# The tail of a graph layer and routed expert kernel: which adds wait for which, dense weights once for two graphs, and the order of the last 50 work items

## The chip, the cores and the metric

The kernel runs on one core of a Trainium2 chip. The metric is the device time of one execution in microseconds (us), as the median of several runs. A profiled execution of the same program is read beside it; all durations below come from that one.

## The reference, cut to what matters

16 graphs of 512 nodes with 128 features go through two residual layers. The first is a graph layer (convolutions along the nodes, an adjacency weighted message sum, gates). The second is a mixture of 8 experts with 2 chosen for each token:

```python
x = x + gnn(layernorm(x), adj, ...)
xn = layernorm(x) * gamma + beta
top_vals, top_idx = top_k(xn @ Wr + br, 2)
w = softmax(top_vals)
for e in range(8):
    h = gelu(xn @ W1[e] + b1[e])          # 128 -> 256
    y = y + (h @ W2[e] + b2[e]) * w_full[..., e]   # 256 -> 128
x = x + y
```

What is added to a token is the weighted output of its two experts.

## The kernel before

An iteration g from 0 to 15 computes the graph layer of graph g and ends that of graph g - 1 (residual sum, norm, router). The first 14 graphs are **routed**: GpSimd (POOL) scatters each token's row, with its weights and its own number, into the regions of its two experts in a DRAM tensor `routed`. Tiles of 256 rows (T0, T1, ...) are read back with the expert's weights, go through the expert, and POOL adds their results into `out` with indirect accumulating DMAs, two for a tile (L943 to L952). From g = 4 on, four such tiles are streamed in each iteration: T0 to T47.

Two tiles may hold the same token, and an accumulating DMA must not run beside another one on the same row. So `add` (L943) waits on POOL for the semaphore `added` to count all adds of all tiles before, for every tile.

The last two graphs (q = 0 and 1) are **dense**: all 8 experts run on all their tokens, and VectorE (DVE) adds weighted results to the graph's tile in SBUF, which SyncE (SP) stores at the end.

After the last iteration comes the **tail**, a list of 50 items that `last_items` (L350) writes out: 18 tiles (T48 to T65, `LAST`) and 32 dense items (graph q, expert e, half u of 256 tokens). Five tiles come first, then two dense items after each tile, then the dense items that are left. Item i passes through the engines as follows: a tile is transposed (`turn`), `hidden` multiplies by W1 on TensorE (PE), ScalarE (ACT) does gelu, `second` multiplies by W2 (L570), ACT adds the bias, `back` transposes, and DVE multiplies by the weights (`weigh`, `dense_weigh`), which raises `y_done`. At step i PE issues turn(i+2), hidden(i+1), second(i), back(i-1). Items alternate between two sets of PSUM banks (bank_set, by the number m of the item): H and Y for even items, G for odd ones.

Tile buffers (`xt`, `w1_t`, `w2_t`, `y_t`) form a ring of 8. The weights of a dense pair of items are in `wd1` and `wd2`, two buffers in turn; there are 16 such loads, one for each graph and expert, and each serves two items. SP issues all loads of the tail in one order that `loads_in_order` (L377) writes out. Before a tile's loads SP reads the tile's place and expert out of SBUF (`choice`, L418 to L420) and waits until the adds of the tile eight before it are done (L481); before a dense load it waits until the items of the load two before it are done (L424 to L426). SP is one queue: what waits there holds up all that follows.

The tables of places come from DVE (`table_steps`, L1157). The tail's own table (`LAST` entries) is made in iteration 15, in `t_start_last` and `t_expert_last`; SP waits for it (L472), stores 8 blocks of pad rows behind the experts' regions (L473 to L475) and then loads T48. With this input, counting the reference's choices, 13 of the 18 tail tiles hold tokens: 2, 1, 2, 1, 1, 2, 2 and 2 for the experts 0 to 7. The other 5 are filled with pad rows.

Of the kernel before, what the change touches and what calls it, by code (L numbers as in the profile page):

```python
# [47 lines left out]
ADD_ITEMS = 3  # L48
# [62 lines left out]
LAST_STEPS = 15  # L111
# [23 lines left out]
def pad_rows():  # L135

    r = np.zeros((SLOTS, TILE, ROW), np.float32)
    r[:, :, R_ID] = (TOKENS + np.arange(TILE)).astype(np.uint32).view(np.float32)
    return r.reshape(SLOTS * TILE, ROW)


def gnn_moe(nc, x, adj_t, weights, vectors, consts, pads, routed, w1_all, w2_all, out):
# [4 lines left out]
    with ExitStack() as ctx:  # L147
# [35 lines left out]
        late_end = sb("late_end", [P, 512])  # L183

# [65 lines left out]

        t_c = sb("t_c", [1, EXPERTS], I32)
# [14 lines left out]
        t_pad = sb("t_pad", [1, EXPERTS], I32)  # L266

# [82 lines left out]
        def last_items():  # L350


            dense = [(q, e, u) for q in range(DENSE) for e in range(EXPERTS) for u in range(NODES // TILE)]
# [10 lines left out]
        items = list(last_items())  # L364

# [25 lines left out]
        def _(sp):  # L391
# [16 lines left out]
            sp.dma_start(routed[DUMMY:DUMMY + SLOTS * TILE, :], pads).then_inc(pads_stored, 16)  # L408
            sp.dma_start(out[TOKENS:TOKENS + TILE, :], pads[0:TILE, 0:P]).then_inc(out_set, 16)
# [8 lines left out]
            def choice(table, i):  # L418
                at = sp.value_load(t_start[table][0:1, i:i + 1], min_val=0, max_val=DUMMY + (SLOTS - 1) * TILE)
                e = sp.value_load(t_expert[table][0:1, i:i + 1], min_val=0, max_val=EXPERTS - 1)  # L420
                return at, e

            def dense_loads(k):
                if k >= 2:  # L424
                    sp.wait_ge(pe_y, last_of_load(k - 2) + 1)
                    sp.wait_ge(yT_done, last_of_load(k - 2) + 1)  # L426
                e = k % EXPERTS
# [49 lines left out]
            sp.wait_ge(pads_stored, 16 * (EXPERTS + 1))  # L477
# [13 lines left out]
            for q in range(DENSE):  # L491
                sp.wait_ge(y_done, last_of_load((q + 1) * EXPERTS - 1) + 1)
# [259 lines left out]
        def _(act):  # L752
# [156 lines left out]
            number = {item[1]: item[0] for item in items if is_tile(item)}  # L909
# [25 lines left out]
        def _(pool):  # L935
# [7 lines left out]
            def add(n, m=None):  # L943
                j = n % RING
                pool.wait_ge(y_done, (n if m is None else m) + 1)
                if n > 0:
                    pool.wait_ge(added, 16 * TT * n)
                for t in range(TT):
# [3 lines left out]
                        in_=y_t[j][:, t, :], in_offset=None, compute_op=ALU.add).then_inc(added, 16)  # L952

            def iteration(g, tail, more, moe):
# [41 lines left out]
            pool.wait_ge(out_set, 16 * (ROUTED + 1))  # L996
            for item in items:
                if is_tile(item):
                    add(item[1], item[0])

        @block.vector
        def _(dve):
# [154 lines left out]
            def table_steps(d, tiles, table):  # L1157
# [18 lines left out]
                def tables(beside):  # L1176
# [7 lines left out]
                    if every:  # L1184
# [12 lines left out]
                                                 over(t_e[:, 0:tiles], 2, s_e1), ALU.is_equal), beside=beside)  # L1197
                    step(nc.vector.tensor_tensor(oh, oh, over(t_z[:], 1, s_e1), ALU.mult), beside=beside)
                    step(nc.vector.tensor_reduce(t_s[:, 0:tiles], oh, AX.X, ALU.add), beside=beside)
                    if every:  # L1200
                        step(nc.vector.tensor_tensor(t_s[:, 0:tiles], t_s[:, 0:tiles], steps, ALU.add), beside=beside)
                        step(nc.vector.tensor_scalar(start[:], t_s[:, 0:tiles], float(DUMMY), None, ALU.min),
                             wait=False)
# [32 lines left out]

            def weigh(n, m=None):
                m = n if m is None else m
                dve.wait_ge(pe_yT, m + 1)
                dve.wait_ge(own_done, n + 1)  # L1240
                nc.vector.tensor_tensor(y_t[n % RING][:],  # L1241
                                        YO[bank_set(m)][:, TILE:2 * TILE].rearrange("p (t d) -> p t d", t=TT),
# [220 lines left out]
            sums = {}  # L1463
            for i in range(-2, len(items) + 1):
                if i + 2 < len(items) and is_tile(items[i + 2]):
                    m, n, j, loads = items[i + 2]
                    tile_lo(n, bank_set(m))
                    own_weight(n, j, loads)
# [87 lines left out]
```

## Time and profile before

| what | value |
|---|---|
| time, median of 3 runs | 682.06 us (680.07 to 682.51) |
| time of the profiled execution | 677.4 us |
| its span in the profile | 675.6 us |
| TensorE busy | 623.9 us (92% of the span) |
| VectorE, ScalarE, GpSimd busy | 493.2, 417.7, 339.4 us |
| adds of tiles on GpSimd (L949) | 132, mean 1623 ns each |
| idle time of GpSimd before them | 189.8 us, of it 98.7 us for an earlier add to land |
| tail, first transpose of T48 to the last transpose | 546.5 to 666.2 us |
| mean granted TensorE clock | 0.98 of full speed |

The span is what the profiler saw of the program's instructions; 1.8 us of the execution lie around it. A line such as L949 is a line of the kernel before. "Releaser" is the instruction or DMA that ended a wait; "issue" is idle time for which the profile shows no releaser.

### The profile page before, as it was taken

The page shows a single profiled execution, that of the slowest core. Times are in us where ns is not written, and L with a number is a line of the kernel's source. Part 1 is how long each engine was busy: PE and PEld are TensorE (multiplying, and loading weights), DVE is VectorE, ACT ScalarE, POOL GpSimd, SP SyncE. Part 2 cuts the span into 40 slices and gives each one's busy share as a digit, 9 for nine tenths or more (in the row PEclk, how much of TensorE's full clock was granted, in tenths as well). Part 3 has the DMA queues.
Part 4 walks back from the last instruction along what each step waited for, and adds up shares of the span by engine and source line. Part 5 has one row for each costly group of instructions (what it writes and reads, how often), then busy time and mean ns, then how long its engine had stood idle before and what let it go on. Part 6 is the DMA issues. An engine that isn't in the chain of part 4 may idle for free.

```text
span 675.6 us, 12962 instructions
## 1 busy us (share of the span) xinstructions
PE 623.9 (92%) x3784; PEld 529.7 (78%) x3784; DVE 493.2 (73%) x2028; ACT 417.7 (62%) x824; POOL 339.4 (50%) x255
## 2 busy tenths in 40 slices
PE   3799897999999999999999999999999988898993
PEld 2779586788888888888888888888888867787872
DVE  6958878778888888888888888888878755333321
ACT  4554445385858585858585858585858556465661
POOL 3100404044757474757484847485748435354554
PEclk9899898999999999999999999999999999899997
DMA  8227231445574757564757565656565586666543
GB/s 299 93 90 251 77 118 50 133 144 159 139 183 126 178 130 180 127 183 124 172 135 177 131 175 132 173 133 175 134 169 137 124 213 156 155 164 160 125 87 60
DMA packets 102710, 99.14 MB, mean 147 GB/s; under 512 B 9056, under 2 KB 80480, under 8 KB 102368
## 3 DMA queue, kind: packets, MB, share of 16 engines
q1 hardware_dynamic: 80048, 81.39, 39.2%
q0 software_dynamic: 22592, 16.92, 16.6%
q8 instruction: 31, 0.51, 0.3%
q14 instruction: 39, 0.32, 0.2%
HBM read 73.97 MB, written 26.21 MB: 148 GB/s over the span
## 4 chain that ended last, share of the span: by engine, by line
PE 80%; DVE 11%; issue 3%; DMA 2%; ACT 2%; POOL 1%; POOLq 0%; SPq 0%; DVEq 0%; ACTq 0%
PE Y L570 9%; PE C L502 9%; PE C L503 8%; PE C L504 8%; PE G L678 7%; PE G L502 5%; PE G L504 4%; PE G L503 4%; PE G L570 3%; PE H L545 2%; PE H L546 2%; PE H L547 2%; PE Y L578 2%; PE G L533 2%; PE M L508 2%
## 5 line engine op out<-in xcount | busy, mean ns | idle before, releaser
L949 POOL DMA_INDIRECT out<-y_t,xt x132 | 214.3, 1623 | 189.8 <-DMA out<-y_t,xt 98.7
L964 POOL DMA_INDIRECT routed<-row,at_u x112 | 116.4, 1040 | 126.8 <-DVE at_u L1152 96.4
L502 PE MATMUL C<-cv_h,w_hi 128*128 128x256 f32 (+1 forms) x432 | 133.2, 308 | 8.9 <-DVE cv_l L1013 7.5
L503 PE MATMUL C<-cv_l,w_hi 128*128 128x256 f32 (+1 forms) x432 | 125.9, 291 | 0.0
L504 PE MATMUL C<-cv_h,w_lo 128*128 128x256 f32 (+1 forms) x432 | 125.5, 290 | 0.0
L502 PEld LDWEIGHTS C<-cv_h,w_hi 128*128 128x128 f32 x432 | 84.1, 195 | 14.9 <-DVE cv_l L1013 9.9
L503 PEld LDWEIGHTS C<-cv_l,w_hi 128*128 128x128 f32 x432 | 84.1, 195 | 1.3
L504 PEld LDWEIGHTS C<-cv_h,w_lo 128*128 128x128 f32 x432 | 84.0, 194 | 0.7
L570 PE MATMUL Y<-ge,w_t 128*128 128x256 f32 x228 | 61.5, 393 | 3.6 <-DVE y_t L1241 1.6
L678 PE MATMUL G<-ex,msg_t 128*128 128x512 f32 x128 | 58.9, 603 | 0.3 <-ACT gh L871 0.3
L570 PEld LDWEIGHTS Y<-ge,w_t 128*128 128x128 f32 x228 | 39.4, 192 | 21.2 <-issue 17.9
L773 ACT ACTIVATE ge<-H,w_t 128x256 f32<-128x256 f32 x114 | 47.8, 472 | 6.0 <-PE H L547 4.2
L678 PEld LDWEIGHTS G<-ex,msg_t 128*128 128x128 f32 x128 | 23.1, 191 | 23.5 <-issue 22.9
L502 PE MATMUL G<-xlT_h,w_hi 128*128 128x512 f32 x96 | 39.9, 415 | 1.5 <-DVE xlT_l L1083 1.5
L880 ACT CAST cv_h<-G 128x512 fp32r<-128x512 f32 x16 | 9.4, 586 | 50.8 <-PE G L678 50.8
L1348 DVE TENSOR_TENSOR ex<-ex,adj 128x512 f32<-128x512 f32 x64 | 39.8, 680 | 0.0
L504 PE MATMUL G<-xlT_h,w_lo 128*128 128x512 f32 x96 | 38.4, 400 | 0.0
L503 PE MATMUL G<-xlT_l,w_hi 128*128 128x512 f32 x96 | 38.1, 396 | 0.0
L545 PE MATMUL H<-xT_h,w_t 128*128 128x256 f32 x114 | 35.8, 314 | 0.7 <-DVE xT_l L1225 0.7
L781 ACT ACTIVATE yT<-Y,w_t 128x256 f32<-128x256 f32 x57 | 27.1, 475 | 11.9 <-PE Y L570 11.0
L1083 DVE TENSOR_TENSOR xlT_l<-M,xlT_h 128x512 fp32r<-128x512 f32 x16 | 11.1, 692 | 30.3 <-ACT xlT_h L801 30.3
L547 PE MATMUL H<-xT_h,w_t 128*128 128x256 f32 x114 | 32.2, 282 | 0.0
(250 smaller groups left out, 1637.6 us busy)
## 6 DMA issues: line engine op xcount, KB each, us to landing
w_t<-w_all SPq DMA_DIRECT2D x66, 256.0 KB, 4.2
adj<-adj_t SPq DMA_DIRECT2D x16, 1024.0 KB, 5.7
xt<-routed SPq DMA_DIRECT2D x66, 144.0 KB, 3.3
w_t<-w_all SPq DMA_DIRECT2D x66, 136.0 KB, 3.7
x_ln<-x SPq DMA_DIRECT2D x16, 256.0 KB, 6.1
x_res<-x SPq DMA_DIRECT2D x16, 256.0 KB, 6.6
wd<-w_all SPq DMA_DIRECT2D x16, 256.0 KB, 3.9
out<-x SPq DMA_DIRECT2D x15, 256.0 KB
```

What stands on the lines that cost most here:

```text
L502: pe.matmul(psum, hi(w), rhs_h, start=start, stop=False)
L503: pe.matmul(psum, hi(w), rhs_l, start=False, stop=False)
L504: return pe.matmul(psum, lo(w), rhs_h, start=False, stop=stop)
L545: pe.matmul(half, w[:, h * P:(h + 1) * P], x_h, start=True, stop=False)
L547: last = pe.matmul(half, w[:, (2 + h) * P:(3 + h) * P], x_h, start=False, stop=True)
L570: last = pe.matmul(YO[bank_set(m)][:, 0:TILE], w2[:, h * P:(h + 1) * P], ge[m % 2][:, h, :], start=(h == 0), stop=(h == HALVES - 1))
L678: last = pe.matmul(G0[:], msg_t[:, j, :], ex[:, j, :], start=(j == 0), stop=(j == NT - 1))
L773: last = nc.scalar.activation(ge[m % 2][:, h, :], HID[bank_set(m)][:, h * TILE:(h + 1) * TILE], ACT.Gelu, bias=w2[:, X_B1 + h:X_B1 + h + 1])
L781: nc.scalar.activation(yT[m % 2][:], YO[bank_set(m)][:, 0:TILE], ACT.Identity, bias=w2[:, X_B2:X_B2 + 1]).then_inc(yT_done, 1)
L949: nc.gpsimd.indirect_dma_start(out=out, out_offset=bass.IndirectOffsetOnAxis(ap=xt[j][:, t, R_ID:R_ID + 1].bitcast(U32), axis=0), in_=y_t[ ...
L964: nc.gpsimd.indirect_dma_start(out=routed, out_offset=bass.IndirectOffsetOnAxis(ap=at_u[:, n:n + 1], axis=0), in_=row[:, n // TOP, :], in_ ...
L1348: nc.vector.tensor_tensor(ex[:, j, :], ex[:, j, :], adj[:, j, :], ALU.mult).then_inc(a_prod, 1)
```

## The change

**Adds wait for other experts' tiles only.** The tail's tiles are in order of their expert. A token is at most once in one expert's region, so two tiles of one expert never touch the same row. In the tail, `last_add` waits for the count of adds that stood before the first tile of its own expert. That count is worked out on DVE (five table steps more and one less, `LAST_STEPS` 19 in place of 15), lies in `t_run`, and POOL reads the 18 values into registers in iteration 15, 9 ahead of the add of T46 and 9 behind it. Before each pair of adds there is a small POOL operation. All pad tiles wait for all real ones. As pad tiles may now be added side by side, they have rows of their own: `pads` grows from 1024 to 4608 rows, and `out` from 256 to 4608 rows behind the tokens. Three quarters of that (3584 rows of 576 bytes in `routed` and 3584 of 512 bytes in `out`) are stored by SP in iteration 5, from DRAM to DRAM.

**Results and row numbers get buffers of their own.** `y_last` gives each of the 18 tiles its own place (in `adj`, `ex` and `x_ln`, which are free by then), and `take_places` on DVE copies a tile's row numbers to `ids`. So the ring's buffers are free once PE, ACT and DVE have read them: from T56 on, SP waits for those in place of the adds.

**Dense weights are loaded once for both graphs.** 10 loads in place of 16: experts 0 and 1 for graph 0, experts 2 to 7 for both graphs (four items each), and experts 0 and 1 for graph 1.

**One and two dense items to a tile in turn.** T65 is item 37 of 0 to 49 (before: item 43), with 12 dense items behind it. The loads of T56 to T60 now stand ahead of the third dense load in SP's order; before it was those of T56 and T57. The lists, with d for a dense item and the number of its load:

```
before: T48 T49 T50 T51 T52 d0 d0 T53 d1 d1 T54 d2 d2 T55 d3 d3 ... T65 d13 d13 d14 d14 d15 d15
after:  T48 T49 T50 T51 T52 d0 d0 T53 d1 T54 d1 d2 T55 d2 T56 d2 d2 ... T65 d6 d6 d6 d6 d7 d7 d7 d7 d8 d8 d9 d9
```

```diff
-ADD_ITEMS = 3
+EARLY = 2
+DENSE_LOADS = ([(e, (0,)) for e in range(EARLY)] + [(e, (0, 1)) for e in range(EARLY, EXPERTS)] +
+               [(e, (1,)) for e in range(EARLY)])
...
-                    for q, e, u in dense[k:k + 2]:
-                        yield m, q, e, u, k // 2
+                    for entry in dense[k:k + 1 + n % 2]:
+                        yield m, *entry
...
-            at = [(last_of_load(k - 2), 1, k) for k in range(2, DENSE * EXPERTS)]
-            at += [(STREAMED + ADD_ITEMS * (n - RING - STREAMED + 1), 0, n) for n in range(STREAMED, STREAMED + LAST)]
+            at = [(last_of_load(k - 2), 1, k) for k in range(2, len(DENSE_LOADS))]
+            at += [(number.get(n - RING, STREAMED), 0, n) for n in range(STREAMED, STREAMED + LAST)]
...
+                if g == FIRST + 1:
+                    sp.dma_start(routed[DUMMY + TAKEN:, :], pads[TAKEN:, :]).then_inc(pads_stored, 16)
+                    sp.dma_start(out[TOKENS + TAKEN:, :], pads[TAKEN:, 0:P]).then_inc(pads_stored, 16)
...
             def last_loads(n):
                 at, e = choice(2, n - STREAMED)
-                sp.wait_ge(added, 16 * TT * (n - RING + 1))
+                if n < STREAMED + RING:
+                    sp.wait_ge(added, 16 * TT * (n - RING + 1))
+                else:
+                    sp.wait_ge(pe_y, number[n - RING] + 1)
+                    sp.wait_ge(yT_done, number[n - RING] + 1)
+                    sp.wait_ge(own_done, n - RING + 1)
...
+            def load_starts(a, b):
+                for i in range(a, b):
+                    run_starts.append(pool.value_load(t_run[0:1, i:i + 1], min_val=16 * TT * STREAMED,
+                                                      max_val=16 * TT * (STREAMED + LAST)))
+            def last_add(n, m):
+                i = n - STREAMED
+                pool.wait_ge(y_done, m + 1)
+                pool.wait_ge(added, run_starts[i])
+                nc.gpsimd.tensor_tensor(pool_spare[:, i:i + 1], cst[:, 0:1], cst[:, 1:2], ALU.add)
+                for t in range(TT):
+                    nc.gpsimd.indirect_dma_start(
+                        out=out, out_offset=bass.IndirectOffsetOnAxis(ap=ids[:, i, t:t + 1], axis=0),
+                        in_=y_last[i][:, t, :], in_offset=None, compute_op=ALU.add).then_inc(added, 16)
...
+                if d == ROUTED:
+                    pool.wait_ge(tab_step, TAB_STEPS * (ROUTED - 2) + LAST_STEPS)
+                    load_starts(0, LAST // 2)
                 tile_add(2)
...
+                if d == ROUTED:
+                    load_starts(LAST // 2, LAST)
...
+                    if every:
+                        step(nc.vector.tensor_tensor(t_f[:, 0:EXPERTS], t_cum[:], t_a[:], ALU.subtract), wait=False)
+                        step(nc.vector.tensor_copy(t_f[:, EXPERTS:], t_cum[:, EXPERTS - 1:]), beside=beside)
+                        step(nc.vector.tensor_tensor(t_of[:], oh, over(t_f[:], 1, s_e1), ALU.mult), beside=beside)
+                        step(nc.vector.tensor_reduce(t_r[:], t_of[:], AX.X, ALU.add), beside=beside)
+                        step(nc.vector.tensor_scalar(t_run[:], t_r[:], 16 * TT / TILE, float(16 * TT * STREAMED), ALU.mult,
+                                                     ALU.add), wait=False)
...
+            def take_places(n, j, loads):
+                dve.wait_ge(xt_in[j], loads)
+                nc.vector.tensor_copy(ids[:, n - STREAMED, :], xt[j][:, :, R_ID].bitcast(U32))
```

## Rows read from the trace of the kernel before

**Rows 1.** The chain that ended last: start us, us, what.

```profile
662.05 1.55 POOL out L949
...
663.91 3.47 DMA out<-y_t,xt
...
668.13 1.55 POOL out L949
```

**Rows 2.** GpSimd in order of time: start us, us; idle time in brackets.

```profile
544.72 1.55 POOL L949 DMA_INDIRECT out<-y_t,xt  x1 [4.01 <-DVE y_t L1241]
...
551.18 1.55 POOL L949 DMA_INDIRECT out<-y_t,xt  x1 [3.06 <-DMA out<-y_t,xt]
```

**Rows 3.** Line L147, sequencers at the end: durations in ns, starts.

```profile
L147 POOLq DRAIN  x1: 7002/7002/7002, 668.4 to 668.4; - x1
```

**Rows 4.** Line L495, SyncE's last wait: when it was over.

```profile
L495 SPq EVENT_SEMAPHORE  x1: 17/17/17, 673.2 to 673.2; - x1
```

**Rows 5.** All engines in order of time, the last microseconds.

```profile
666.35 0.61 DVE L1255 SCALAR_TENSOR_TENSOR x<-G,w_d,x 128x128 f32<-128x128 f32 x2 [0.17 <-PE G L578]
666.99 0.39 SPq L493 DMA_DIRECT2D out<-x  x1
```

**Rows 6.** SyncE in order of time, a graph's store in iteration 14.

```profile
486.50 0.40 SPq L447 DMA_DIRECT2D out<-x  x1
```

**Rows 7.** GpSimd in order of time, the add that this store released.

```profile
488.67 1.64 POOL L949 DMA_INDIRECT out<-y_t,xt  x1 [0.30 <-DMA out<-x]
```

**Rows 8.** SyncE in order of time, its issues at the tail's start.

```profile
540.05 0.41 SPq L412 DMA_DIRECT2D xt<-routed  x1
...
556.52 0.38 SPq L412 DMA_DIRECT2D xt<-routed  x1
...
570.57 0.38 SPq L412 DMA_DIRECT2D xt<-routed  x1
...
572.09 0.37 SPq L428 DMA_DIRECT2D wd<-w_all  x1
```

**Rows 9.** VectorE in order of time, the tail's table in iteration 15.

```profile
524.26 0.32 DVE L1198 TENSOR_TENSOR t_oh<-t_oh,t_z 1x162 f32<-1x162 f32 x1
...
524.61 0.31 DVE L1199 TENSOR_REDUCE t_s<-t_oh 1x18 f32<-1x162 f32 x1
```

**Rows 10.** TensorE in order of time, idle times ahead of dense items.

```profile
576.22 0.55 PE L545 MATMUL G<-xd_h,wd 128*128 128x256 f32 x1 [1.76 <-issue]
...
610.86 0.36 PE L545 MATMUL H<-xd_h,wd 128*128 128x256 f32 x1 [0.95 <-issue]
...
631.12 0.36 PE L545 MATMUL G<-xd_h,wd 128*128 128x256 f32 x1 [0.76 <-issue]
...
659.07 0.35 PE L545 MATMUL H<-xd_h,wd 128*128 128x256 f32 x1 [0.73 <-issue]
```

**Rows 11.** Windows: PE, PEld, DVE, ACT, POOL busy us; PEclk, DMA share, GB/s.

```profile
577.00:578.00 1.00, 1.00 (x5) 0.97 (x5) 0.00 (x0) 0.07 (x1) 0.17 (x1) 0.50 0.07 16
```

**Rows 12.** Line L419, SyncE's reads of the table: ns.

```profile
L419 SPq TENSOR_LOAD <-t_start_last x18: 262/272/279, 538.7 to 620.7; - x18
```

**Rows 13.** GpSimd's groups: busy us, mean ns | idle us before.

```profile
L989 POOL TENSOR_TENSOR rs<-ve,cst 128x4 f32<-128x4 f32 x1 | 1.0, 1018 | 2.1 <-DVE ve L1036 2.1
```

**Rows 14.** Page, part 3: queue, packets, MB, share of 16 engines.

```profile
q1 hardware_dynamic: 80048, 81.39, 39.2%
```

**Rows 15.** Windows of iterations 5 and 6, columns as in Rows 11.

```profile
203.00:209.00 6.00, 5.86 (x31) 4.73 (x31) 4.07 (x12) 4.56 (x9) 4.24 (x5) 1.00 0.73 216
209.00:215.00 6.00, 6.00 (x48) 5.67 (x47) 5.73 (x12) 5.05 (x11) 5.09 (x4) 1.00 0.29 37
```

**Rows 16.** SyncE in order of time, tile loads of iteration 6.

```profile
230.54 0.39 SPq L412 DMA_DIRECT2D xt<-routed  x1
```

**Rows 17.** DMA issues in 11 to 30 us: KB, us to landing.

```profile
routed<-pads SPq DMA_DIRECT2D x1, 576.0 KB, 10.1
```

**Rows 18.** DMA issues in 526 to 540 us.

```profile
routed<-pads SPq DMA_DIRECT2D x8, 144.0 KB, 2.5
```

More of the change, by code:

```diff
@@ L248, in gnn_moe @@
         at_u = sb("at_u", [P, NT * 2], U32)
+        y_last = [tile[:, t, h * TILE:(h + 1) * TILE].rearrange("p (t d) -> p t d", t=TT)
+                  for tile in (adj, ex) for t in range(NT) for h in range(NODES // TILE)]
+        y_last += [x_ln[:, t:t + TT, :] for t in range(0, NT, TT)]
+        ids = sb("ids", [P, LAST, TT], U32)
         t_c = sb("t_c", [1, EXPERTS], I32)
@@ L266, in gnn_moe @@
         t_pad = sb("t_pad", [1, EXPERTS], I32)
+        t_f = sb("t_f", [1, EXPERTS + 1])
+        t_of = sb("t_of", [1, LAST, EXPERTS + 1])
+        t_r = sb("t_r", [1, LAST])
+        t_run = sb("t_run", [1, LAST], I32)
         parts = {
@@ L350, in last_items @@
         def last_items():
-            dense = [(q, e, u) for q in range(DENSE) for e in range(EXPERTS) for u in range(NODES // TILE)]
+            dense = [(q, e, u, k) for k, (e, graphs) in enumerate(DENSE_LOADS) for q in graphs
+                     for u in range(NODES // TILE)]
             m, n, k = STREAMED, STREAMED, 0
@@ L359, in last_items @@
                 if n > STREAMED + SPACED or n == STREAMED + LAST:
-                    for q, e, u in dense[k:k + 2]:
-                        yield m, q, e, u, k // 2
+                    for entry in dense[k:k + 1 + n % 2]:
+                        yield m, *entry
                         m, k = m + 1, k + 1
         items = list(last_items())
+        number = {item[1]: item[0] for item in items if len(item) == 4}
         def bank_set(m):
@@ L418, in choice @@
             def choice(table, i):
-                at = sp.value_load(t_start[table][0:1, i:i + 1], min_val=0, max_val=DUMMY + (SLOTS - 1) * TILE)
+                at = sp.value_load(t_start[table][0:1, i:i + 1], min_val=0, max_val=DUMMY + (LAST - 1) * TILE)
                 e = sp.value_load(t_expert[table][0:1, i:i + 1], min_val=0, max_val=EXPERTS - 1)
@@ L491, in _ @@
             for q in range(DENSE):
-                sp.wait_ge(y_done, last_of_load((q + 1) * EXPERTS - 1) + 1)
+                sp.wait_ge(y_done, max(item[0] for item in items if not is_tile(item) and item[1] == q) + 1)
                 sp.dma_start(out_v[ROUTED + q], x1_d[q][:]).then_inc(out_set, 16)
@@ L908, in _ @@
             results(STREAMED - 1, w2_t[(STREAMED - 1) % RING])
-            number = {item[1]: item[0] for item in items if is_tile(item)}
             for i in range(-2, len(items)):
@@ L941, in w_lo_part, with add @@
                                         ALU.subtract).then_inc(w_lo_done[name], 1)
-            def add(n, m=None):
+            def add(n):
                 j = n % RING
-                pool.wait_ge(y_done, (n if m is None else m) + 1)
+                pool.wait_ge(y_done, n + 1)
                 if n > 0:
@@ L996, in _ @@
             pool.wait_ge(out_set, 16 * (ROUTED + 1))
+            pool.wait_ge(pads_stored, 16 * (EXPERTS + 3))
             for item in items:
                 if is_tile(item):
-                    add(item[1], item[0])
+                    last_add(item[1], item[0])
         @block.vector
@@ L1200, in tables @@
                     if every:
-                        step(nc.vector.tensor_tensor(t_s[:, 0:tiles], t_s[:, 0:tiles], steps, ALU.add), beside=beside)
-                        step(nc.vector.tensor_scalar(start[:], t_s[:, 0:tiles], float(DUMMY), None, ALU.min),
-                             wait=False)
+                        step(nc.vector.tensor_tensor(start[:], t_s[:, 0:tiles], steps, ALU.add), wait=False)
                         assert done[0] == LAST_STEPS
@@ L1463, in _ @@
             sums = {}
+            dve.wait_ge(pe_nmp, GRAPHS)
             for i in range(-2, len(items) + 1):
@@ L1467, in _ @@
                     tile_lo(n, bank_set(m))
+                    take_places(n, j, loads)
                     own_weight(n, j, loads)
@@ L1548 @@
     args = [nc.dram_tensor(n, t.shape, F32, kind="ExternalInput").ap() for n, t in arrays.items()]
-    routed = nc.dram_tensor("routed", (DUMMY + SLOTS * TILE, ROW), F32, kind="Internal").ap()
+    routed = nc.dram_tensor("routed", (DUMMY + LAST * TILE, ROW), F32, kind="Internal").ap()
     w1_all = nc.dram_tensor("w1_all", (EXPERTS, P, W1COLS), F32, kind="Internal").ap()
     w2_all = nc.dram_tensor("w2_all", (EXPERTS, P, XCOLS), F32, kind="Internal").ap()
-    out = nc.dram_tensor("out", (TOKENS + TILE, P), F32, kind="ExternalOutput").ap()
+    out = nc.dram_tensor("out", (TOKENS + LAST * TILE, P), F32, kind="ExternalOutput").ap()
     gnn_moe(nc, *args, routed, w1_all, w2_all, out)
```

22 lines of the change are left out of this document (12 added, 10 removed).

## The prediction

> **What bounds the kernel now.** I read the chain that ended last from its end, then the engines' order of time over the tail. The span does not end with arithmetic. VectorE ends its last dense item at 666.35 + 0.61 = 666.96 us, and SyncE stores the graph at 666.99 [rows 5]. The chain's last links are adds on GpSimd: issue, 3.47 us until it lands, the next tile's issue at 668.13 [rows 1]. GpSimd's sequencer then sits in its final drain until 668.4 + 7.0 = 675.4 [rows 3], 2.2 us after SyncE's own last wait at 673.2 [rows 4], and the span ends at 675.6. So the end is set by a string of adds in which each waits for the one before: T47's starts at 551.18 [rows 2] and T65's at 668.13 [rows 1], so 18 tiles take 116.95 us, 6.50 us each. Behind this, by only 6 us, runs a second bound: TensorE with the 50 items. It is busy nearly all the time, but it stands still ahead of some dense items: 1.76 us at 576.22, then 0.95 and 0.76 us with two more (0.48 and 0.55 us) between them, and 0.73 us near the end [rows 10]. The profile calls these "issue". I read them as waits for dense weights: the first ends at 576.22, 4.1 us after SyncE issued that load at 572.09 [rows 8, 10], and four of the others come behind a dense load that stood in SyncE's queue behind a tile's load, which waited for adds.
>
> **The change part by part.** All sums are made against the profiled execution: 677.4 us, span 675.6. The median of the runs shown is 682.06, 4.7 us above it; I take the difference in span over to the median as it is.
>
> *Adds.* With this input 9 tiles of 18 begin an expert's run or the pad tiles (T48, T50, T51, T53, T54, T55, T57, T59, T61) and still wait, at 6.50 us each. The other 9 need only POOL's own time, two issues of 1.55 us with 0.3 us ahead of each, 3.7 us. From T47's 551.18 that is 9 x 6.50 + 9 x 3.7 = 91.8 us: T65's add at 643.0 at the earliest. The small operation ahead of each pair is not in the trace; it lies between 0 and the 1.02 us of a POOL operation on 128x4 [rows 13], so up to 18 us more, 661. T65's result itself is 12 items from the end, so at about 666.96 - 12 x 2.09 = 641.9 (the pace is worked out below). From T65's issue to the end of the drain were 675.4 - 668.13 = 7.3 us [rows 1, 3]; so GpSimd is through between 650 and 668 us. That leaves the end to the dense chain: last store at 666.99, landed at most 2.17 us later (the store at 486.50 released an add that started at 488.67 [rows 6, 7]; there are five such pairs, all 2.16 to 2.18), and about 0.3 us for SyncE to leave: 669.5. **First term: 669.5 - 675.6 = -6.1 us**, if TensorE's timetable stays.
>
> *The order of loads.* It does not stay. The third dense load is needed by item 11 in both lists. It is now behind the loads of T48 to T60, 13 tiles, where it was behind 10. Unhindered, SyncE starts a tile's loads each (556.52 - 540.05)/6 = 2.745 us, and the dense load follows the last tile's start by 572.09 - 570.57 = 1.52 us [rows 8]. The start moves too: SyncE waits for the tail's table, and DVE's net four steps more cost about 0.35 us for each of the two large ones (524.61 - 524.26 [rows 9]) and 0.15 for the small ones, 0.85 us in all. So the dense load goes at 540.05 + 0.85 + 12 x 2.745 + 1.52 = 575.4, plus 0.33 us that T55 takes beyond the pace and some 0.1 us for the added waits of each of five tiles: 576.2 in place of 572.09. The old queue had waited for adds, the new one runs at its own issue rate. **Second term: +4.1 us**: TensorE resumes at 580.3 and not at 576.2. All small delays ahead of it (the table, five copies of row numbers on DVE) end in this same wait and cost nothing more. The clock was granted at 0.50 just behind the 1.76 us stop [rows 11], that is 1.2 GHz, from 575.9 to 579.1; I expect the same dip behind a stop of about 5 us, no longer once work is back. That half microsecond more or less goes to the range.
>
> *Fewer dense loads.* From item 11 on each load serves four items and has four to eight items of lead, and tile loads no longer wait for adds. The four stops of 0.95, 0.48, 0.55 and 0.76 us go. **Third term: -2.7 us.** The one of 0.73 us stays, as the last load still waits for the items two loads before and serves the last two. Late next is then TensorE itself: 13 items from 631.12 to 659.07 without the 0.73 are 27.2 us, 2.09 us each [rows 10]; tile and dense items cost about the same, so the new mixture moves nothing.
>
> *Small things on the way.* `take_places` (18 copies of 128x2, 0.17 us each like `own_weight`'s) lies in DVE's idle time, about half of the tail. The wait for `pe_nmp` is for something 10 us old. Reading 18 values into registers on POOL: SyncE's read takes 0.27 us [rows 12], and about 0.58 with what follows it, so 5.3 us for nine. POOL idles 4.0 us ahead of T46's add and 3.1 us ahead of T47's [rows 2]. If the sequencer reads while the engine still makes descriptors, as its drain begins at 668.4 [rows 3] while the last issue starts only at 669.99, both batches hide. If not, T46's add moves 1.6 us and T47's about 4; T55's load waits for T47's add, and the second term grows by about 2. I take 0 and keep 2 for the range. On this the Trainium skill (Advanced Engine Details and Errata, Sequencer and Instruction Queues) says that other engine instructions can be read and queued while a control instruction executes; the drain's start speaks for the same. *Pads in iteration 5*: 3584 x (576 + 512) bytes are 3.9 MB. The queue's average is 0.392 x 675.6/81.39 = 3.25 us of all 16 engines for a MB [rows 14], so 12.7 us. Behind 203 us the engines are 73% and then 29% taken [rows 15], so 5.9 us are free in 12, and the rest fits in some 10 more; the next tile loads come at 230.5 [rows 16]. I take 0.3 us for this and DVE's extras together.
>
> **Sum**: -6.1 + 4.1 - 2.7 + 0.3 = -4.4 us. Span 671.2, its execution 673.0, median 677.6.
>
> **The rivals.**
> *A. The burst costs nothing.* If the third dense load lands in time for its old place, by a faster read of the table and shorter landings, the second term is 0: -8.5 us, 673.5. Against it: SyncE's pace is the most regular number in the tail. Chance 0.12.
> *B. The burst and the registers cost more*, the reads on POOL are not hidden and dense weights land later in the fuller traffic: second term 6 to 8 us, result -2.5 to -0.5, say 680.5. Chance 0.22. The same result comes if the adds still end last, as they would with 1.1 us or more for POOL's small operation.
> *C. Slower: the copies in iteration 5.* They go into the queue that carries all loads. At the average cost they fit. But the one copy of this kind at the start took 10.1 us for 576 KB [rows 17]; at that rate 3.9 MB take 66 us. Much of those 10.1 us was the queue ahead of it, since 144 KB land in 2.5 us [rows 18]. It decides from the point where the copies still run at 230.5, 27 us after their issue, when the tiles of the next iteration stand behind them; a copy of 45 us would stop TensorE some 15 us once, -4.4 + 15 = +10.6, 692.7. The Trainium skill (DMA: Bandwidth & Descriptors, Issuing engines are not separate DMA queues) says that all DMAs run on the same 16 engines and interleave, so POOL's adds would suffer with the loads. No row here shows such a large copy. Chance 0.08.
> *D. The adds do not get ahead*: the registers hold the count of all tiles, so that nothing is thinned. Then 18 x 6.50 us stay, only T65's result is earlier, and the end stays at about 675: 682. Chance 0.03.
>
> **How the numbers follow.** Forecast -4.4 us with 0.55, its own range from -7 to -2.5 (675.1 to 679.6) by the bounds of landing, clock and registers. A, B, C, D with 0.12, 0.22, 0.08 and 0.03. The range 673.5 to 681.5 takes in the forecast, A and most of B. A measurement of this kernel tells about 0.5% (3.4 us) from no change, so the line lies at 678.6. Faster: A and three quarters of the forecast, 0.55. Slower: C, 0.08. The rest 0.37.
>
> **What would show it.** After the change the chain that ended last must hold no add behind the last dense item, and GpSimd must be idle for some 10 us before the end. TensorE's stop ahead of item 11 should read about 5 us with the dense load issued near 576, and the stops near 610 to 631 should be gone. POOL's pairs should stand 3.7 us apart for T49, T52, T56, T58, T60 and T62 to T65, where results are there. Windows of iterations 5 and 6 should show more GB/s and the same TensorE share. The prediction is wrong if TensorE stops elsewhere in the tail, or if anything before 540 us grows.

## The result and the profile after the change

The median went from 681.23 to 678.15 us, ratio 0.995 with a 95% interval of 0.993 to 0.997: 3.1 us by the medians, 3.4 us by the ratio. The forecast was 677.6 us, 4.4 us less than before. The profiled execution of the changed kernel took 676.38 us with a span of 674.6 us, only 1.0 us less than the span of before, 675.6. One of the 15 executions of each kernel was far slower than the rest (713.74 and 883.57 us), and the ratio leaves both out. That the two profiles show a third of what the medians show is taken up below.

I read the end first. The changed kernel's engines in order of time, GpSimd's last add and the last microseconds:

```profile
651.24 1.56 POOL L997 DMA_INDIRECT out<-x_ln,ids  x1 [0.30 <-issue]
...
671.24 0.61 DVE L1318 SCALAR_TENSOR_TENSOR x<-G,w_d,x 128x128 f32<-128x128 f32 x2 [0.17 <-PE G L606]
671.88 0.39 SPq L521 DMA_DIRECT2D out<-x  x1
```

The final drains of its line L150 (the L147 of before; durations in ns, starts):

```profile
L150 POOLq DRAIN  x1: 11169/11169/11169, 646.2 to 646.2; - x1
...
L150 SPq DRAIN  x1: 7/7/7, 674.4 to 674.4; - x1
```

The last add is issued nearly 21 us before the last store, and GpSimd's drain is over at 646.2 + 11.2 = 657.4, 17 us ahead of the end. Before, this drain ended the span [rows 3]. Now the span ends 2.7 us behind the last store; before it ended 8.6 us behind it [rows 5]. The chain that ended last goes through TensorE's items up to this end, and from the stop on it holds no add:

```profile
579.62 3.13 issue
584.37 1.71 PE Y L598 x4
...
644.38 1.10 PE Y L598 x4
669.03 1.12 PE G L598 x4
```

The same chain shows what the change cost. SyncE in order of time, the tail's first load and those of T60 and the third dense load:

```profile
543.07 0.41 SPq L431 DMA_DIRECT2D xt<-routed  x1
...
576.69 0.38 SPq L431 DMA_DIRECT2D xt<-routed  x1
578.21 0.38 SPq L447 DMA_DIRECT2D wd<-w_all  x1
578.64 1.90 SPq L448 DMA_DIRECT2D wd<-w_all  x1
```

TensorE in order of time, T47's second product and the stops:

```profile
547.23 1.10 PE L598 MATMUL Y<-ge,w_t 128*128 128x256 f32 x4 [1.21 <-DVE y_t L1305]
...
582.75 0.55 PE L573 MATMUL G<-xd_h,wd 128*128 128x256 f32 x1 [3.13 <-issue]
...
663.83 0.36 PE L573 MATMUL H<-xd_h,wd 128*128 128x256 f32 x1 [0.91 <-issue]
```

T60's load goes at 576.69, the third dense load right behind it at 578.21, and TensorE starts item 11 at 582.75, 4.5 us after that issue. Between that stop and the one at 663.83 there is no other with "issue" behind it: the four that stood from 610 to 632 us before [rows 10] are gone. Windows around the stop show the half clock (columns as in rows 11), first in the changed kernel, then in before around its stop at 576.22:

```profile
575.00:580.00 5.00, 4.45 (x30) 3.73 (x28) 2.21 (x6) 2.97 (x7) 1.39 (x3) 1.00 0.93 238
580.00:585.00 5.00, 2.25 (x8) 2.12 (x9) 0.74 (x4) 0.57 (x3) 4.23 (x5) 0.65 0.86 195
585.00:590.00 5.00, 5.00 (x25) 4.38 (x23) 2.67 (x22) 2.58 (x7) 1.25 (x2) 0.67 0.94 232
```

```profile
575.00:580.00 5.00, 3.78 (x17) 3.39 (x18) 0.21 (x1) 1.31 (x3) 1.86 (x2) 0.66 0.54 119
580.00:585.00 5.00, 4.22 (x28) 3.57 (x27) 3.72 (x28) 2.86 (x8) 1.81 (x2) 1.00 0.67 156
```

The last three numbers are the granted clock as a share of full speed, the DMA share and GB/s. A mean of 0.65 and 0.67 between the levels 1.00 and 0.50 is 3.5 + 3.3 = 6.8 us at half clock; before it was 3.4 us. The changed kernel has another 3.4 us at half clock from 567.9 us on, ahead of the stop. They cost it nothing by the reading here, since item 11 waits for its weights in any case.

And GpSimd in order of time: the adds of T57, which begins an expert's run, and the first of T58, which does not.

```profile
613.28 0.19 POOL L995 TENSOR_TENSOR pool_spare<-cst 128x1 f32<-128x1 f32 x1 [1.76 <-DMA out<-ex,ids]
613.93 1.55 POOL L997 DMA_INDIRECT out<-ex,ids  x1 [0.46 <-issue]
615.79 1.55 POOL L997 DMA_INDIRECT out<-ex,ids  x1 [0.30 <-issue]
616.80 0.79 POOL L995 TENSOR_TENSOR pool_spare<-cst 128x1 f32<-128x1 f32 x1
617.76 1.56 POOL L997 DMA_INDIRECT out<-ex,ids  x1 [0.17 <-issue]
```

From 613.93 to 617.76 are 3.8 us where the tile does not wait. The small operation takes 0.19 us behind a wait, with 0.46 us more until the issue; without a wait its 0.79 us are over (617.59) hardly later than the issue before it (615.79 + 1.55 = 617.34). The nine tiles that go on with an expert's run or with the pad tiles (T49, T52, T56, T58, T60 and T62 to T65) all start 3.8 us behind the tile before them, where the prediction had 3.7.

**A ruler for the tail.** Executions differ by some microseconds ahead of the tail, so spans don't show an edit of 4 us. The kernel of e2, described below, has the tail of the kernel before, item for item, so its profile is a third one of that tail. I measure each profile from S, the start of T47's second product on TensorE (the line with the idle time of 1.21 us), in three stretches: S to R, TensorE's start of item 11; R to the last store; that store to the end of the span (spans are read to 0.1 us).

| profile | S | S to R | R to store | store to end | S to end |
|---|---|---|---|---|---|
| before | 544.59 | 31.63 | 90.77 | 8.61 | 131.0 |
| before, again (e9) | 547.08 | 32.17 | 91.35 | 9.70 | 133.2 |
| copies alone (e2) | 544.61 | 30.80 | 90.44 | 8.65 | 129.9 |
| changed | 547.23 | 35.52 | 89.13 | 2.72 | 127.4 |
| changed, again (e5) | 550.29 | 36.88 | 88.47 | 2.66 | 128.0 |

The order of loads is that of the changed kernel in e3 and e4 too; S to R is 34.9 and 36.8 us there.

### The profile page after: what moved, and what is told of

Read it like the earlier page. It is cut to its first block, busy times and chain, and to the rows that moved or that the text cites. A ratio compares the mean times of both kernels' runs of the same rounds, so it can differ in the third digit from the quotient of the medians.

```text
span 674.6 us, 13053 instructions
## 1 busy us (share of the span) xinstructions
PE 626.7 (93%) x3784; PEld 531.7 (79%) x3784; DVE 497.3 (74%) x2050; ACT 418.0 (62%) x824; POOL 345.8 (51%) x273
## 4 chain that ended last, share of the span: by engine, by line
PE 72%; DVE 10%; issue 5%; DMA 5%; ACT 3%; POOL 2%; SPq 1%; another core or an unknown queue 1%; POOLq 0%; DVEq 0%; ACTq 0%
PE Y L598 10%; PE C L530 7%; PE C L532 7%; PE C L531 7%; PE G L706 5%; PE G L530 4%; PE G L532 4%; PE G L531 4%; PE G L598 4%; DMA out<-y_t,xt 3%; PE H L573 2%; PE Y L606 2%; PE H L575 2%; PE H L574 2%; PE M L536 2%
## 5 line engine op out<-in xcount | busy, mean ns | idle before, releaser
L976 POOL DMA_INDIRECT out<-y_t,xt x96 | 159.0, 1656 | 131.6 <-DMA out<-y_t,xt 82.6
L1011 POOL DMA_INDIRECT routed<-row,at_u x112 | 118.3, 1056 | 124.6 <-DVE at_u L1205 91.7
L573 PE MATMUL H<-xT_h,w_t 128*128 128x256 f32 x114 | 36.1, 317 | 0.8 <-DVE xT_l L1284 0.8
L574 PE MATMUL H<-xT_l,w_t 128*128 128x256 f32 x114 | 32.4, 284 | 0.0
```

Of the source, the lines that this page charges most:

```text
L573: pe.matmul(half, w[:, h * P:(h + 1) * P], x_h, start=True, stop=False)
L574: pe.matmul(half, w[:, h * P:(h + 1) * P], x_l, start=False, stop=False)
L976: nc.gpsimd.indirect_dma_start(out=out, out_offset=bass.IndirectOffsetOnAxis(ap=xt[j][:, t, R_ID:R_ID + 1].bitcast(U32), axis=0), in_=y_t[ ...
L1011: nc.gpsimd.indirect_dma_start(out=routed, out_offset=bass.IndirectOffsetOnAxis(ap=at_u[:, n:n + 1], axis=0), in_=row[:, n // TOP, :], in_ ...
```

## The experiments

The theory was the sum of the prediction: the end passes to the dense chain, and a part of that gain is given back because the third dense load stands behind 13 tile loads. The rivals: the gain or the loss comes from the copies in iteration 5, from the adds alone, from the number of dense loads, or from the new order of items. The first four ran on one chip, beside the kernel before (median 679.09 us there).

**e1_order.** The changed kernel with four tile loads moved behind the third dense load.

```diff
-            at += [(number.get(n - RING, STREAMED), 0, n) for n in range(STREAMED, STREAMED + LAST)]
+            at += [(number.get(n - RING, STREAMED) if not 56 < n < 61 else last_of_load(0) + 0.5, 0, n)
+                   for n in range(STREAMED, STREAMED + LAST)]
```

> The changed kernel with the loads of T57 to T60 behind the third dense load and not ahead of it. Theory (the burst of tile loads ahead of that load stops TensorE): the load, issued at 578.2 in the changed kernel, goes at about 568 to 569, TensorE's stop of 3.13 us ahead of item 11 and the half clock behind it are gone, and the time falls by 3.1 + 1.3 = 4.4 us against the changed kernel, so the ratio to the kernel before is about 0.989. Rival (the stop is something else, such as instruction fetch, and only coincides with the load): the stop stays at 2 to 3 us and the ratio stays at 0.995.

Measured: 669.88 us, ratio 0.986 (0.984 to 0.989), span 667.9. SyncE's third and fourth dense load, in order of time:

```profile
570.12 0.34 SPq L448 DMA_DIRECT2D wd<-w_all  x1
...
588.67 0.36 SPq L448 DMA_DIRECT2D wd<-w_all  x1
```

TensorE's stops with "issue" behind them from 570 us on:

```profile
593.04 0.36 PE L574 MATMUL H<-xd_h,wd 128*128 128x256 f32 x1 [1.01 <-issue]
...
657.07 0.36 PE L574 MATMUL H<-xd_h,wd 128*128 128x256 f32 x1 [0.94 <-issue]
```

The third dense load goes 25.0 us behind S (545.14), where it was 31.0, and item 11 starts without a stop. The next dense load, now behind the moved tile loads, costs 1.01 us (2.41 us in e10, the same kernel again). From S to the end are 122.8 us in place of 127.7 (mean of the two profiles of the changed kernel). The second term is real, the order of SyncE's loads alone makes it, and it can be had back. How much that is worth differs with the ruler: 4.9 us by these stretches, 6.0 us by the ratios here (0.995 to 0.986), and 3.3 and 3.5 us with e10.

**e2_copies.** The kernel before with the large `pads` and the two copies in iteration 5 alone.

```diff
+                if g == FIRST + 1:
+                    sp.dma_start(routed[DUMMY + TAKEN:, :], pads[TAKEN:, :]).then_inc(pads_stored, 16)
+                    sp.dma_start(out[TOKENS + TAKEN:, :], pads[TAKEN:, 0:P]).then_inc(pads_stored, 16)
```

> The kernel before with the larger pads alone: the two DRAM to DRAM copies of 3.9 MB in iteration 5, and the wait for them at the tail. Theory (they fit into free DMA time): iterations 5 and 6 grow by 0.7 us at most, ratio 1.000 to 1.001. Rival (the copies are what moved the changed kernel's tail 2.6 us later in its profile): ratio 1.004.

Measured: 678.79 us, ratio 1.000 (0.998 to 1.002). Windows of iterations 5 and 6:

```profile
203.00:209.00 6.00, 5.85 (x32) 4.77 (x31) 4.06 (x9) 4.54 (x9) 4.78 (x5) 1.00 1.11 341
209.00:215.00 6.00, 5.92 (x47) 5.53 (x47) 5.83 (x13) 4.95 (x11) 4.96 (x4) 1.00 0.99 317
215.00:221.00 6.00, 6.00 (x49) 5.83 (x48) 5.75 (x44) 5.94 (x10) 4.90 (x4) 1.00 1.14 320
221.00:227.00 6.00, 6.00 (x43) 5.46 (x41) 4.93 (x12) 3.48 (x10) 3.32 (x3) 1.00 0.40 78
```

The copies fill the DMA engines for some 18 us at over 300 GB/s and are through by about 221, 9 us before the next tile loads; TensorE's busy time (the first behind the comma) is that of before within 0.1 us [rows 15]. Rival C falls. At the rate of the copy at the start, the prediction had 66 us for them; they took 18.

This profile also gives the third row of the old tail above. TensorE's start of item 11:

```profile
575.41 0.36 PE L548 MATMUL G<-xd_h,wd 128*128 128x256 f32 x1 [0.96 <-issue]
```

**e3_all_adds.** The changed kernel, but each tile's adds wait for all adds before them.

```diff
-                pool.wait_ge(added, run_starts[i])
+                pool.wait_ge(added, 16 * TT * n)
```

> The changed kernel, but each tail add waits for the adds of all tiles before, as in the kernel before; buffers, order and loads stay changed. Theory (only the thinned waits take the adds off the end): 18 tiles at 6.50 us plus about 0.65 for the small operation, so from T48's 560.8 the last add starts near 682 and the span ends near 689, 14 us later than the changed kernel, ratio about 1.016. Rival (the earlier place of T65 and the freed buffers alone would have done): ratio within 0.002 of the changed kernel's 0.995.

Measured: 678.04 us, ratio 1.000 (0.997 to 1.002): the gain is gone, but it is not a loss of 1.6% as I had expected of it. The end of GpSimd and its drain:

```profile
667.66 0.19 POOL L995 TENSOR_TENSOR pool_spare<-cst 128x1 f32<-128x1 f32 x1 [1.76 <-DMA out<-x_ln,ids]
668.31 1.56 POOL L997 DMA_INDIRECT out<-x_ln,ids  x1 [0.46 <-issue]
670.17 1.56 POOL L997 DMA_INDIRECT out<-x_ln,ids  x1 [0.30 <-issue]
```

```profile
L150 POOLq DRAIN  x1: 7011/7011/7011, 668.5 to 668.5; - x1
```

I had counted the small operation on top of each pair. From T47's add at 552.41 to T65's at 668.31 a tile took 6.44 us here, no more than the 6.50 of before [rows 1, 2]. The adds end last again, by 4 us (store to end 6.9 us), and 130.1 us from S are 2.4 more than with the thinned waits. So in this kernel the thinned waits themselves are worth 2.4 us by these stretches and 3.2 us by the ratios. That there is no more for them to free because the dense chain is late by its own load is what e7 tests.

**e4_16_loads.** The changed kernel with 16 dense loads, one for each graph and expert.

```diff
-DENSE_LOADS = ([(e, (0,)) for e in range(EARLY)] + [(e, (0, 1)) for e in range(EARLY, EXPERTS)] +
-               [(e, (1,)) for e in range(EARLY)])
+DENSE_LOADS = [(e, (q,)) for q in range(DENSE) for e in range(EXPERTS)]
```

> The changed kernel with a dense load for each graph and expert again (16 in place of 10), each serving two items. Theory: in the middle of the tail a load has about 6 us of lead against 4 us to land and costs nothing, but the 12 dense items behind T65 now meet a stop of some 0.9 us at each pair, five or six of them in place of one: +3.5 to +4.5 us against the changed kernel, ratio about 1.000. Rival (one load for two graphs saves nothing as loads were hidden): ratio 0.995.

Measured: 677.57 us, ratio 0.997 (0.996 to 0.999). TensorE, its stops with "issue" behind 600 us:

```profile
650.91 0.36 PE L572 MATMUL H<-xd_h,wd 128*128 128x256 f32 x1 [1.71 <-issue]
656.00 0.36 PE L572 MATMUL H<-xd_h,wd 128*128 128x256 f32 x1 [0.87 <-issue]
661.00 0.36 PE L572 MATMUL H<-xd_h,wd 128*128 128x256 f32 x1 [0.78 <-issue]
666.05 0.36 PE L572 MATMUL H<-xd_h,wd 128*128 128x256 f32 x1 [0.84 <-issue]
```

R to the last store is 91.7 us, against 88.8 in the mean of the changed kernel: the shared loads are worth 2.9 us in this stretch. The ratios say 1.2 to 1.6 us, less than the 3.5 to 4.5 expected, and their intervals overlap. The stops are not those of before: they stand behind T65, where only dense items are left, one at each load of two items, which waits for the items two loads before it. The four of before stood between 610 and 632 us, where tile loads waited for adds. They do not come back with 16 loads: from 583 to 650 us this profile has no stop with "issue" behind it. So it was not the number of loads that removed them; the shared loads only spare the tail the stops that its new order, with 12 dense items at the end, would have. That the four went because tile loads no longer wait for adds is what is left; no run puts that wait back alone.

The next four ran on a second chip (before: 682.15 us there).

**e5_again.** The changed kernel, nothing edited, for a second profile and a ratio of its own.

> The changed kernel as it is, once more, on the same chip as the runs beside it. Theory (the 3 us that its first profile lost in iteration 4, ahead of the tail, are a mishap of that execution, as the runs with the same copies and the same code up to the tail lost 0.2 to 1.0 us): iterations up to 15 lie within 1 us of the kernel before, TensorE's stop ahead of item 11 is 3 to 6 us, ratio 0.993 to 0.995. Rival (it is the changed kernel's own): the 3 us are there again at 157 to 193 us.

Measured: 679.40 us, ratio 0.996 (0.993 to 0.999). The 3 us of iteration 4 are there again (35.4 us between the two adjacency loads that are shown under e9), so the expected text's theory of a mishap fell. The dense load is issued at 583.51 us, 36.8 us behind T48's, and the stop reads 5.75 us:

```profile
587.17 0.55 PE L573 MATMUL G<-xd_h,wd 128*128 128x256 f32 x1 [5.75 <-issue]
```

**e6_two_dense.** e1 with two dense items behind each tile, as before the change.

```diff
-                    for entry in dense[k:k + 1 + n % 2]:
+                    for entry in dense[k:k + 2]:
```

> The kernel of e1_order (dense load ahead of T57 to T60) with two dense items behind each tile, as in the kernel before, so T65 is item 43 again and has 6 items behind it. Theory (with thinned waits the adds need only about 8 us behind T65's result, and 6 items give 12.5): ratio as e1_order, 0.986 within 0.0025. Rival (the alternation is what takes the adds off the end): adds end last again, 2 to 5 us more, ratio 0.989 to 0.993.

Measured: 675.26 us, ratio 0.989 (0.985 to 0.992). From S to the end are 123.8 us, as in the two profiles of e1's order (122.8 and 124.4). The last add is issued at 660.78, 109.6 us behind S where it is 106.4 in e10. Its issue is over 9 us ahead of the store at 671.61, and GpSimd's drain 4.7 us. The span ends 3.4 us behind the store, 0.7 more than in e1 and e10, and nothing here says why. The new mixture of items makes no difference that these runs can tell.

**e7_order_all_adds.** e1 with the wait for all adds (the edit of e3).

> The kernel of e1_order, but each tail add waits for all adds before. Theory (the two bounds lie side by side, so that freeing one brings little): GpSimd's string of 18 adds at 6.4 us ends where it ended in e3_all_adds, span 675, ratio 0.999, 9 us slower than e1_order. Rival (the load order alone brings the gain): ratio 0.986 to 0.990.

Measured: 684.93 us, ratio 1.004 (1.001 to 1.007), S to end 130.3 us. GpSimd and its drain:

```profile
675.13 1.56 POOL L998 DMA_INDIRECT out<-x_ln,ids  x1 [0.46 <-issue]
676.99 1.56 POOL L998 DMA_INDIRECT out<-x_ln,ids  x1 [0.30 <-issue]
```

```profile
L150 POOLq DRAIN  x1: 7012/7012/7012, 675.4 to 675.4; - x1
```

The order of e1 is worth nothing while the adds are last: 130.3 us from S, against 130.1 in e3. With both, 123.6 (mean of e1 and e10). The thinned waits are worth 6.7 us where the loads are in order and 2.4 us where they are not. Two bounds lie side by side, and each edit alone pays only the distance to the other. The times say the same in kind and more in size: 684.93 us is 9.7 us above e6, whose tail is as short as that of e1, on the same chip, and 0.4% above the kernel before, where 0.1% below was expected. Of the 9.7 us some 6.4 lie between S and the end, and 1.2 ahead of S, where the two kernels do the same work; the rest lies between the profiled executions and the medians, and what causes it is open.

**e8_both_ends.** e1, with T60 to T62 behind the fourth dense load, and experts 6 and 7, shared by both graphs, as the last two loads.

```diff
-DENSE_LOADS = ([(e, (0,)) for e in range(EARLY)] + [(e, (0, 1)) for e in range(EARLY, EXPERTS)] +
-               [(e, (1,)) for e in range(EARLY)])
+DENSE_LOADS = ([(e, (0,)) for e in range(EARLY)] + [(e, (0, 1)) for e in range(EARLY, EXPERTS - 2)] +
+               [(e, (1,)) for e in range(EARLY)] + [(e, (0, 1)) for e in range(EXPERTS - 2, EXPERTS)])
...
-            at += [(number.get(n - RING, STREAMED), 0, n) for n in range(STREAMED, STREAMED + LAST)]
+            at += [(number.get(n - RING, STREAMED) if not 56 < n < 63 else last_of_load(n // 60) + 0.5, 0, n)
+                   for n in range(STREAMED, STREAMED + LAST)]
```

> The kernel of e1_order with two more edits: the loads of T60 to T62 go behind the fourth dense load, and the two single-graph loads of graph 1 stand ahead of experts 6 and 7, so that the last loads serve four items each. Theory: TensorE's stop of 1.01 us ahead of item 17 and that of 0.94 us near the end (the last load waited for items only two items back) are gone, 1.9 us less than e1_order, ratio 0.983. Rival (the end stop only moves to the weights of another load): ratio 0.986.

Measured: 672.85 us, ratio 0.985 (0.982 to 0.989), S to end 121.0 us, the shortest of all. Neither of the two stops of e1 is left; one of the same size stands earlier, near the loads of experts 0 and 1 for graph 1, which serve two items each:

```profile
647.54 0.36 PE L574 MATMUL H<-xd_h,wd 128*128 128x256 f32 x1 [0.89 <-issue]
```

Both kernels are beaten, by 1.5% and 1.0%. Against e1 (0.986 on its chip, 0.990 below) it is not told apart by the ratios. Its tail is shorter than both of e1's order, 121.0 us against 122.8 and 124.4, but that is one profile, and those two differ by 1.6 us.

**e9_before_again and e10_order_again**, on a third chip (before: 683.43 us there): the kernel before and the kernel of e1, neither edited. The question was why the profile of the changed kernel begins its tail 2.6 us later than that of before, and why the median of before lay 4.7 us above its profiled execution.

> The kernel before, unchanged. In the profiled execution of before TensorE's work after 157 us runs some 2.5 to 3 us earlier than in the profiles of the changed kernel and of three other variants, though nothing in the change acts between 157 and 193 us. Theory 1: this is a state of an execution and not of a kernel. Then a second profile of before is as likely as not to show it too: its adjacency load of iteration 5 would be issued 2.5 us later than 190.3 minus the old profile's place, its first tile load of the tail near 543 us in place of 540.05, its span near 678. Theory 2: it comes from the changed program (its length or its places in memory). Then the first tile load of the tail is at 540.05 within 0.3 us again. Timed, the ratio must hold 1.000.

> The changed kernel with the loads of T57 to T60 behind the third dense load, unchanged from e1_order, whose profile had no loss between 157 and 193 us and a ratio of 0.986. If that loss is a state of an execution, the ratio is 0.986 again (0.982 to 0.990) whether or not this profile shows it; if e1_order had been lucky and the order of loads is worth less than the 4.1 us of the second term, the ratio lies at 0.990 or above. The stop ahead of item 11 must be absent in either case.

Measured: 682.53 us, ratio 1.000 (0.997 to 1.003), for the kernel before, and 674.89 us, ratio 0.990 (0.982 to 0.997), for e1's order. That ratio lies on the border between the two readings of the expected text, and its interval holds both; the stop ahead of item 11 is absent, as expected. SyncE's adjacency loads of iterations 4 and 5, first in before, then in before again, and GpSimd's add just ahead of the second of them in before again:

```profile
157.50 0.39 SPq L450 DMA_DIRECT2D adj<-adj_t  x1
...
190.34 0.39 SPq L450 DMA_DIRECT2D adj<-adj_t  x1
```

```profile
157.29 0.39 SPq L450 DMA_DIRECT2D adj<-adj_t  x1
...
193.34 0.39 SPq L450 DMA_DIRECT2D adj<-adj_t  x1
...
191.05 3.71 POOL L949 DMA_INDIRECT out<-y_t,xt  x1 [2.48 <-DMA out<-y_t,xt]
```

The same program has 32.8 us between these loads in one execution and 36.1 us in the other, and in the second the issue of one add occupies GpSimd for 3.71 us where others take 1.6. The twelve profiles fall into two groups with nothing between: 32.8 to 33.0 us in before and in the four of the first chip, 35.4 to 36.1 us in the changed kernel's profile and in the six of the second and third. So the profile of before happened to be one without this loss, and the changed kernel's one with it. It is not the clock: the granted clock is 1.00 from 150 to 200 us in all twelve. With before again in place of before, the gain of 1.0 us between the spans becomes 5.7 us, 680.3 to 674.6. Of the 4.7 us between the two executions of before, 2.5 lie ahead of S and 2.2 behind it, in the tail, so this pair overstates the gain as the other understates it.

## Why the prediction was right, point by point

**First term** (the end passes to the dense chain; -6.1 us). Held. The stretch from the last store to the end of the span went from 8.61 and 9.70 us to 2.72 and 2.66, so -6.5 us in the mean (-6.3 with e2's 8.65). The term had assumed 669.5 - 666.99 = 2.5 us behind the store. GpSimd was expected through by 650 to 668 us; it was at 657.4.

**Second term** (the third dense load behind the burst; +4.1 us). Held, with a wider scatter than I allowed for. S to R grew from 31.63 and 32.17 to 35.52 and 36.88 us, +4.3 in the mean and anywhere from 3.4 to 5.3 for a pair; with e2, e3 and e4 it is 31.5 to 36.0, +4.5. The issue comes 578.21 - 543.07 = 35.1 us behind T48's load, where I had 576.2 - 540.9 = 35.3, and TensorE resumes 4.5 us later, where I had 4.1. In changed again these are 36.8 and 3.7 us. T48's load itself is issued 0.8 us later against S in the mean of two profiles each (4.54 and 4.72 us ahead of S, then 4.16 and 3.56), where I had 0.85 for the longer table. "The same dip of the clock" was wrong. It was 3.4 us long, to about 579.2, and is 6.8 us long now, to about 588.3 (windows above). From R on TensorE works 5.6 us at 1.2 GHz and not 3.0; by my estimate the extra 2.6 us at half speed cost about 1.3 us behind R. In changed again most of the dip lay within the longer stop, and R was followed by 3.4 us at half clock.

**Third term** (four stops gone; -2.7 us). The four stops are gone, and the stretch from R to the store is 2.3 us shorter in the mean (90.77 and 91.35 to 89.13 and 88.47; 2.1 with e2's 90.44). Of the two reasons that I gave, loads for four items and tile loads that no longer wait for adds, e4 rules out the first: with 16 loads the four do not come back. The second was not tested alone. The 2.3 us contain the clock's cost, up to 1.3 us, and the stop near the end, which stayed as predicted and reads 0.91 us in place of 0.73.

**Small things.** The small POOL operation lies at the low end of the 0 to 1.02 us that I had bounded it by. The register reads do not show: T46's and T47's adds, at 547.36 and 554.25, follow idle times of 4.02 and 3.47 us, where 4.01 and 3.06 stood before [rows 2], T46's starts 0.13 us behind S, as before, and the profile has T47's wait for the landing of an earlier add. The copies in iteration 5 cost nothing that e2 can tell. That the reads ran while the engine made descriptors is my reading, and no run took them away. The Trainium skill (Advanced Engine Details and Errata, Sequencer and Instruction Queues) says that other engine instructions can be read and queued while a control instruction executes. The two gaps do not speak against it, but it is not quite this case, in which the reads run beside an issue that began before them.

**The sum.** From S to the end the means of two profiles each fell by 4.4 us (132.1 to 127.7); predicted were -4.7 for the three terms and -4.4 with the small things. That the two agree so closely is in part luck, as single stretches differ by 1 to 2 us between executions: with e2 as a third profile of the old tail the fall is 3.7 us (131.4 to 127.7). The medians say -3.1 to -3.4. So some 0.3 to 1.3 us may be lost ahead of S. The same-chip pairs point that way too: S at 544.61 in e2, at 545.14 to 545.73 in e1, e3 and e4; 547.08 in before again, 549.26 in e10. A part of it is there by the adjacency load of iteration 4 (157.33 in e2, 157.72 to 158.47 in the others of its chip), well ahead of the copies; yet the changed kernel's own profile has 157.19. What costs it was not settled. I had named growth of anything ahead of 540 us as a sign of being wrong, and this may be such a growth, if a small one. One candidate that I left out of the sum is the larger copy to `out` at the start, 512 KB in place of 128; no run took it away.

**One step of the prediction was lucky.** I carried a difference in span over to the median "as it is", although the median lay 4.7 us above the profiled execution. The median of the changed kernel did come out near it, but I had not asked where the 4.7 us were. A median of 679.1 us on the chip whose profiles lack the loss of iteration 4, and of 682.2 and 683.4 us on the two whose profiles have it, suggests that it makes up most of the 4.7 us and is in the medians of both kernels; no run shows it for the 15 executions of each. A slip in the chances was without effect: 0.12 and three quarters of 0.55 are 0.53 for "faster", where I wrote 0.55.

## What to carry to other kernels

When one queue issues the loads of two streams, an edit that frees one stream from its waits lets it run ahead of the other: count how many issues now stand before each load that somebody is already waiting for, and put that load first. Two bounds a few microseconds apart must be moved together; here, from S to the end, thinned waits were worth 2.4 us alone, load order nothing alone, and both together 6.5 us (130.1 to 123.6). And compare profiles by stretches between marks that the edit cannot touch, since two executions of one program here differed by 4.7 us in span, more than the change was worth.

## What the runs showed of the hardware

- GpSimd's final drain ends 3.8 us after the last accumulating add's issue is over, in nine of the twelve profiles (4.2, 4.6 and 4.6 us in e5, the changed kernel and e6). Its length in the profile is no price: it starts ahead of the last issue (668.4 against 669.99 in before) and is 7.0 us long in the five profiles whose adds end last, and 8.4 to 16.5 us in the others. Where the adds end last, the drain is over 2.0 to 2.2 us after SyncE has seen the last add landed ([rows 3, 4] for before). That is what it costs on top of the landing.
- How long TensorE's half clock lasts does not follow the length of the stop. It was 3.4 us behind stops of 1.57 us (e3), 1.76 and 2.95 us (before, before again), 6.8 us behind 3.13 and 5.75 us (changed, changed again) and 6.24 us (e4), and there was none behind the 2.41 us at 598.90 in e10 (granted clock 1.00 from 575 to 614 us):

```profile
598.90 0.36 PE L574 MATMUL H<-xd_h,wd 128*128 128x256 f32 x1 [2.41 <-issue]
```

A wait of the same size for ScalarE early in the tail was followed by none in before (2.24 us, at 563.89) and by 3.4 us in the changed kernel (2.27 us, at 567.20). A stop can be worth more than its length: by estimate 1.5 us on top for 3.0 us of work at 1.2 GHz.
- One program has two timetables between 157 and 193 us, 2.4 to 3.3 us apart. At the end of the longer one a GpSimd issue takes 3.1 us (changed), 3.7 us (before again) and 1.8 to 1.9 us in four others, but 1.57 us in e10, no more than in before, so that long issue is not what makes it. It went with the chip in all ten profiles whose chip is known; what it is stays open.
